# Grouped whitening in one pass: centring y on its mean over all samples before the gram, against correcting for the mean in the solve

## The reference

```python
y = gn(x)                       # per sample, 32 groups of 4 channels: (v - mean) / sqrt(var + 1e-5)
xf = transpose(y, (1, 0, 2, 3)).reshape(128, M)          # M = 32*56*56
mu = mean(xf, axis=1);  xc = xf - mu
xg = xc.reshape(16, 8, M)                                # 16 groups of 8 channels
cov = einsum('gim,gjm->gij', xg, xg) / M + 1e-4 * eye(8)
e, v = eigh(cov);  proj = v @ diag(rsqrt(e)) @ v.T       # the inverse square root
out = x + (proj @ xg).reshape(C, M) * weight + bias      # back in NCHW
```

## Time and profile before

| | |
|---|---|
| median of 3 runs | 427.79 us (425.38 to 430.95) |
| profiled execution, its own time | 428.58 us |
| its span, first to last instruction | 426.8 us |
| mean granted TensorE clock | 0.994 of full speed |
| bytes moved by DMA | 103.76 MB, mean 243 GB/s |

### The profile page before, as it was taken

How to read it: one execution, slowest core, us unless ns; L and a number is a source line. 1 busy time by engine, 2 the same in 40 slices (tenths; PEclk the granted TensorE clock), 3 DMA queues, 4 the chain that set the end, 5 groups by cost and what they waited for, 6 DMA issues and landing times.

```text
span 426.8 us, 9162 instructions
## 1 busy us (share of the span) xinstructions
PE 359.5 (84%) x3394; PEld 226.6 (53%) x3394; DVE 337.5 (79%) x885; ACT 327.4 (77%) x513; POOL 300.3 (70%) x196
## 2 busy tenths in 40 slices
PE   0124667999999999999999999999999999999991
PEld 0013555565656656655666565656565656555450
DVE  2689999689899999999999999999999885732000
ACT  1065766498989898998989898989898989865462
POOL 0079999387888979797878787878787888930000
PEclk9999999999999999999999999999999999999997
DMA  6999999247766975787776877677866999373657
GB/s 224 275 327 332 315 302 299 80 152 213 236 229 231 294 219 180 243 277 225 229 244 221 294 231 233 233 257 258 283 222 214 328 340 330 121 229 130 226 178 274
DMA packets 18892, 103.76 MB, mean 243 GB/s; under 512 B 6432, under 2 KB 6432, under 8 KB 14752
## 3 DMA queue, kind: packets, MB, share of 16 engines
q1 hardware_dynamic: 18848, 103.19, 74.2%
HBM read 51.78 MB, written 51.38 MB: 242 GB/s over the span
## 4 chain that ended last, share of the span: by engine, by line
PE 47%; POOL 19%; DVE 14%; ACT 8%; issue 6%; SPq 3%; DMA 1%; DVEq 0%
PE ps_apply L564 32%; POOL hl_ring L330 15%; PE ps_small L564 7%; PE ps_gram L564 5%; DVE a_t L445 5%; POOL ring L322 5%; ACT hl_ring L516 4%; ACT ring L525 3%; SPq L286 3%; PE ps_stat L564 3%; DVE bn L346 3%; DMA ring<-in_x_dram 1%; DVE t_ring L392 1%; DVE entries L441 1%; DVE var L362 1%
## 5 line engine op out<-in xcount | busy, mean ns | idle before, releaser
L330 POOL TENSOR_TENSOR hl_ring<-ring,hl_ring 128x768 f16<-128x768 f32 (+1 forms) x128 | 236.4, 1860 | 52.3 <-ACT hl_ring L516 52.2
L564 PE MATMUL ps_apply<-ring,a_t 128*128 128x392 f32 x512 | 203.3, 522 | 0.0
L516 ACT CAST hl_ring<-ring 128x768 f16<-128x768 f32 (+1 forms) x128 | 135.4, 1075 | 10.9 <-POOL ring L322 10.3
L525 ACT ACTIVATE ring<-ps_apply,fin_add,scale 128x784 f32<-128x784 f32 x128 | 126.2, 996 | 20.8 <-PE ps_apply L564 20.7
L346 DVE BATCH_NORM_STATS2 bn<-ring 128x6 f32<-128x448 f32 x224 | 128.7, 595 | 9.8 <-DMA ring<-in_x_dram 9.8
L392 DVE STREAM_TRANSPOSE t_ring<-hl_ring 128x768 f32<-128x768 f32 (+1 forms) x128 | 125.9, 984 | 3.6 <-POOL hl_ring L330 2.0
L564 PEld LDWEIGHTS ps_apply<-ring,a_t 128*128 128x128 f32 x512 | 88.0, 191 | 42.3 <-ACT ring L525 2.3
L564 PE MATMUL ps_gram<-t_ring 128*128 128x64 f16 x1568 | 74.6, 200 | 16.9 <-DVE t_ring L392 16.9
L322 POOL TENSOR_SCALAR ring<-ring,y_mul,y_add 128x832 f32<-128x832 f32 x64 | 66.8, 1044 | 25.8 <-DVE dr L384 25.1
L564 PEld LDWEIGHTS ps_gram<-t_ring 128*128 128x128 f16 x1568 | 61.6, 103 | 26.7 <-DVE t_ring L392 18.3
L504 ACT ACTIVATE ring<-ring,y_add,y_mul 128x768 f32<-128x768 f32 x64 | 65.3, 1020 | 0.0
(11 more groups left out here) (65 smaller groups left out, 228.8 us busy)
## 6 DMA issues: line engine op xcount, KB each, us to landing
ring<-in_x_dram SPq DMA_DIRECT2D x256, 196.0 KB, 3.7
out_dram<-ring SPq DMA_DIRECT2D x128, 392.0 KB, 5.0
cst<-const_dram SPq DMA_DIRECT2D x1, 392.0 KB
wb<-in_L_conv_weight_dram SPq DMA_DIRECT2D x1, 0.5 KB
wb<-in_L_conv_bias_dram SPq DMA_DIRECT2D x1, 0.5 KB
```

The costliest lines, as they stand in the source:

```text
L330: nc.gpsimd.tensor_tensor(hl[:, :, 0], ring[:, g % RING, s, px], hl[:, :, 1], ALU.subtract).then_inc(l_ready, 1)
L516: nc.scalar.copy(hl_ring[:, i % HL_RING, 0:width(p), 1], ring[:, g % RING, s, px]).then_inc(h_ready, 1)
L525: nc.scalar.activation(ring[:, g % RING, s, px].rearrange("p (a b) -> p a b", a=2), ps_apply[:, i % 2 * 2:i % 2 * 2 + 2, 0:BANK], ACT.Iden ...
L564: return nc.tensor.matmul(out_, lhsT, rhs, start=start, stop=stop, skip_group_check=True)
```

## The change

The mean of y over all samples is computed before y is made. It needs only the rows' means: `dr` is multiplied by a new constant matrix `every`, which sums over all rows of the same channel modulo 8 and gives each row its channel's mean. The new step `centre` subtracts it from the shift of y (`y_add`) and makes the result's bias `fin_add` at once. With y centred, `HOP_MU`, `HOP_SHIFT`, the `wmu` product and the mean's outer product in `HOP_COV` go; 19 hops are left. `HOP_COV` leaves a plain 8x8 matrix and the first step builds the 16-row layout from it with four products of 8 rows (`cov` and `p0` padded with zeros, `eye`). The addition of the identity writes PSUM (`s_entries`), and `a_t` is expanded from there. All lists of ticks are other ones.

```diff
-ROWS, DEV, VAR, VAREPS, SCALED, Y_SET, STAT_OPS = 2, 3, 6, 7, 10, 12, 13
+ROWS, DEV, VAR, VAREPS, SCALED, DR, Y_SET, STAT_OPS = 2, 3, 6, 7, 10, 13, 14, 15
-BN_AT = [-64, -60, -56, -51, -44, -42, -37, -33, -31, -23, -19, -18, -18, -14]
+BN_AT = [-65, -59, -54, -50, -44, -41, -35, -32, -32, -25, -21, -21, -15, -11]
 MEAN_PE_AT = 1
-DEV_AT = 2
-VAR_PE_AT = 4
-VAREPS_AT = 6
-ROOT_AT = 8
-SCALE_AT = 13
-Y_POOL = {0: 18, 2: 19, 4: 47, 6: 56}
-Y_ACT = {1: 28, 3: 38, 5: 56, 7: 70}
-H_AT = [20, 32, 40, 42, 44, 56, 71, 77]
-L_AT = [31, 42, 48, 49, 50, 69, 75, 82]
-T_AT = [36, 42, 50, 60, 70, 75, 83, 95]
-GRAM_AT = [41, 47, 56, 65, 72, 79, 87, 96]
+DEV_AT = 3
+VAR_PE_AT = 5
+VAREPS_AT = 7
+ROOT_AT = 9
+SCALE_AT = 14
+MU_AT = 16
+CENTRE_AT = 20
+Y_POOL = {0: 9, 2: 23, 4: 47, 6: 66}
+Y_ACT = {1: 21, 3: 33, 5: 47, 7: 72}
+H_AT = [27, 31, 40, 42, 52, 53, 74, 80]
+L_AT = [19, 28, 31, 50, 58, 68, 71, 81]
+T_AT = [36, 44, 52, 65, 70, 79, 84, 96]
+GRAM_AT = [41, 48, 57, 65, 73, 80, 88, 100]
-HOP_AT = [95, 103, 108, 111, 115, 117, 124, 129, 132, 136, 140, 145, 151, 152, 156, 160, 166, 168, 170, 178, 185]
+HOP_AT = [103, 106, 110, 115, 121, 124, 129, 131, 135, 138, 144, 147, 150, 154, 159, 166, 169, 171, 177]
-HOP_READ_AT = [102, 106, 110, 114, 115, 122, 126, 130, 134, 138, 141, 146, 150, 154, 158, 162, 168, 169, 174, 179,
-               188]
+HOP_READ_AT = [104, 108, 115, 116, 123, 127, 130, 134, 139, 142, 146, 152, 154, 159, 162, 166, 169, 174, 181]
-APPLY_AT = [189, 196, 206, 212, 219, 229, 236, 244]
-FINISH_AT = [197, 200, 207, 220, 223, 238, 241, 260]
-STORE_AT = [222, 262]
+APPLY_AT = [192, 198, 206, 213, 220, 229, 236, 248]
+FINISH_AT = [196, 205, 211, 222, 228, 235, 241, 255]
+STORE_AT = [224, 257]
...
+    put("every", (p[:, None] % CG == p[None] % CG) / N)
...
-                nc.vector.scalar_tensor_tensor(out=y_add[:, i], in0=s_mean, scalar=-1.0, in1=y_mul[:, i],
+                nc.vector.scalar_tensor_tensor(out=y_shift[:], in0=s_mean, scalar=-1.0, in1=y_mul[:, i],
                                                op0=ALU.mult, op1=ALU.mult).then_inc(stat_step, 1)
-                nc.vector.tensor_tensor(dr[:, i], dev, y_mul[:, i], ALU.mult).then_inc(stat_step, 1)
+                nc.vector.tensor_tensor(dr[:], dev, y_mul[:, i], ALU.mult).then_inc(stat_step, 1)
+
+            def centre(g):
+                i = g % STAT_RING
+                dve.wait_ge(stat_mm, STAT_MMS * g + 3)
+                mu = s_mu.broadcast_to([P, TILES])
+                nc.vector.tensor_tensor(y_add[:, i], y_shift[:], mu, ALU.subtract).then_inc(stat_step, 1)
+                nc.vector.scalar_tensor_tensor(out=fin_add[:, i], in0=mu, scalar=1.0, in1=scale[:, i],
+                                               op0=ALU.mult, op1=ALU.mult).then_inc(centred, 1)
+                dve.wait_ge(centred, g + 1)
+                nc.vector.tensor_tensor(fin_add[:, i], fin_add[:, i], base[:], ALU.add).then_inc(stat_step, 1)
...
-                    nc.vector.tensor_copy(wmu[:, e], s_wmu[e]).then_inc(solve_read[e], 1)
                     dve.wait_ge(a_step, MATRIX_STEPS * g + 2)
-                    nc.vector.tensor_tensor(entries[:, 1], entries[:, 0],
-                                            k_("id8").unsqueeze(1).broadcast_to([P, TILES, CG]),
+                    whole = s_entries[e].rearrange("p (s c) -> p s c", s=TILES)
+                    nc.vector.tensor_tensor(whole, entries[:], k_("id8").unsqueeze(1).broadcast_to([P, TILES, CG]),
                                             ALU.add).then_inc(a_step, 1)
                     dve.wait_ge(a_step, MATRIX_STEPS * g + 3)
                     nc.vector.tensor_tensor(a_t[:, e].rearrange("p s (n c) -> p s n c", c=CG),
-                                            entries[:, 1].unsqueeze(2).broadcast_to([P, TILES, SAMPLES, CG]),
+                                            whole.unsqueeze(2).broadcast_to([P, TILES, SAMPLES, CG]),
...
+            def mean_of_rows(g):
+                pe.wait_ge(stat_step, STAT_OPS * g + DR)
+                for s in range(TILES):
+                    ins = product(s_mu, k_("every"), dr[:, s:s + 1], s == 0, s == TILES - 1)
+                ins.then_inc(stat_mm, 1)
...
+                if k == HOP_COV:
                     if g >= 2:
-                        pe.wait_ge(fin_ready, g - 1)
+                        pe.wait_ge(a_step, MATRIX_STEPS * (g - 1))
                     pe.wait_ge(gram_reduced, g + 1)
+                    product(s_cov[e], k_("sel"), g_red[:, e], True, False)
+                    ins = product(s_cov[e], g_red[:, e], k_("sel"), False, True)
+                if k == HOP_WV[0]:
+                    c, p = cov[:, e], p0[:, e]
+                    product(s_w[e], c[:, CG:], p[:, 0:CW], True, False)
+                    product(s_w[e], eye[:, 0:CW], p[:, CG:], False, True)
+                    product(s_v_[e], eye[:, CG:], p[:, 0:CW], True, False)
+                    ins = product(s_v_[e], c[:, 0:CW], p[:, CG:], False, True)
```

More of the change, by code:

```diff
@@ L52 @@
 ITERS = len(POLY)
[L57 to L62, removed]
+HOP_COV = 0
+HOP_M = [None] + [2 * k for k in range(1, ITERS)]
+HOP_WV = [2 * k + 1 for k in range(ITERS)]
+HOP_T = 2 * ITERS
+HOP_V, HOP_ROOT = HOP_T + 1, HOP_T + 2
+HOPS = HOP_T + 3
 READS = HOPS - 1
 CW = 2 * CG
-ROWS, DEV, VAR, VAREPS, SCALED, Y_SET, STAT_OPS = 2, 3, 6, 7, 10, 12, 13
+ROWS, DEV, VAR, VAREPS, SCALED, DR, Y_SET, STAT_OPS = 2, 3, 6, 7, 10, 13, 14, 15
@@ L95 @@
+APPLY_AT = [192, 198, 206, 213, 220, 229, 236, 248]
+FINISH_AT = [196, 205, 211, 222, 228, 235, 241, 255]
+STORE_AT = [224, 257]
 LOAD_AT = [STORE_AT[s] + 24 - RING * TICKS for s in range(TILES)]
-FIRST_TICK, LAST_TICK = -TICKS, TICKS * (GROUPS - 1) + 264
+FIRST_TICK, LAST_TICK = -65, TICKS * (GROUPS - 1) + 259
 COLS = {}
 _at = 0
-for _name, _w in (("avg", P), ("bmask", P), ("gmask", UNIT), ("sel", 8 * CG), ("id8", CG),
-                  ("means", 11 * CG), ("expand", P), ("eps", CG), ("eye15", CG), ("wv0", 2 * CW),
+for _name, _w in (("avg", P), ("bmask", P), ("gmask", UNIT), ("sel", CG), ("id8", CG),
+                  ("every", P), ("expand", P), ("eps", CG), ("eye", 3 * CG), ("eye15", CG),
@@ L120, in constants @@
         / (N * HW * Y_SCALE ** 2))
-    sel = np.zeros((P, 8 * CG))
-    sel[:, 3 * CG:4 * CG] = sel[:, 4 * CG:5 * CG] = ch[:, None] % CG == np.arange(CG)[None]
-    put("sel", sel)
+    put("sel", ch[:, None] % CG == np.arange(CG)[None])
     put("id8", p[:, None] % CG == np.arange(CG)[None])
[L125 to L129, removed]
+    put("every", (p[:, None] % CG == p[None] % CG) / N)
     put("expand", p[None] % CG == np.arange(CG)[:, None])
@@ L180, in zca_residual @@
         zx = sb("zx", [CG, 2, P])
-        wmu = sb("wmu", [CG, 2, 1])
-        entries = sb("entries", [P, 2, TILES, CG])
+        entries = sb("entries", [P, TILES, CG])
         a_t = sb("a_t", [P, 2, TILES, P])
-        fin_add = sb("fin_add", [P, 2, TILES])
+        fin_add = sb("fin_add", [P, STAT_RING, TILES])
         ps_apply = ps("ps_apply", [P, 4, 512])
@@ L403, in gram_sum @@
                 dve.wait_ge(gram_masked, g + 1)
-                blocks = g_red[:, g % 2, 3 * CG:5 * CG].rearrange("p (b i) -> p b i", i=CG)
-                nc.vector.tensor_reduce(blocks, g_masked[:].rearrange("p (n i) -> p i n", i=CG).unsqueeze(
-                    1).broadcast_to([P, 2, CG, CG]), AX.X, ALU.add).then_inc(gram_reduced, 1)
+                nc.vector.tensor_reduce(g_red[:, g % 2], g_masked[:].rearrange("p (n i) -> p i n", i=CG),
+                                        AX.X, ALU.add).then_inc(gram_reduced, 1)
             def read_hop(g, k):
@@ L449, in read_hop @@
                                             ALU.mult).then_inc(a_step, 1)
[L450 to L454, removed]
             def read_weights():
                 dve.wait_ge(wb_product, 1)
-                nc.vector.tensor_scalar(wb[:, :, 0], s_wb[:, 0:GROUPS], -1.0 / TRACE ** 0.5, None, ALU.mult)
-                nc.vector.tensor_scalar(wb[:, :, 1], s_wb[:, 0:GROUPS], 1.0 / (Y_SCALE * TRACE ** 0.5), None,
+                nc.vector.tensor_scalar(wb[:, :, 0], s_wb[:, 0:GROUPS], 1.0 / (Y_SCALE * TRACE ** 0.5), None,
                                         ALU.mult).then_inc(w_scaled, 1)
-                nc.vector.tensor_copy(wb[:, :, 2], s_wb[:, GROUPS:2 * GROUPS])
+                nc.vector.tensor_copy(wb[:, :, 1], s_wb[:, GROUPS:2 * GROUPS])
                 dve.wait_ge(w_scaled, 1)
-                nc.vector.tensor_tensor(id8w[:], wb[:, :, 1].unsqueeze(2).broadcast_to([P, GROUPS, CG]),
+                nc.vector.tensor_tensor(id8w[:], wb[:, :, 0].unsqueeze(2).broadcast_to([P, GROUPS, CG]),
                                         k_("id8").unsqueeze(1).broadcast_to([P, GROUPS, CG]),
                                         ALU.mult).then_inc(wb_ready, 1)
-            nc.vector.memset(g_red[:], 0.0).then_inc(zeros_set, 1)
+            nc.vector.memset(cov[:], 0.0)
+            nc.vector.memset(p0[:], 0.0).then_inc(zeros_set, 1)
```

(11 more changed lines are left out.)

73 lines of the change are left out of this document (27 added, 46 removed).

## The result

The changed kernel takes 449.19 us (447.98 to 449.89) against 426.95 beside it, ratio 1.0503 [1.0424, 1.0581]. Forecast were 412 us and 404 to 423. The profiled execution took 449.57 us with a span of 447.8.

What follows compares the result with a forecast made beforehand. Bound: the chain of waits through `a_t`, 22.39 us a period, with TensorE nearly full. 22.39 - 1.63 + 0.5 gave 21.3, larger than TensorE's 20.86; 13.1 us over 12 periods, 15.9 in total, hence 412 us, range 404 to 423.

Steps and rivals of the forecast that it cites:

- `a_t` from PSUM: VectorE's expansion into `a_t`, with one PSUM input, escapes the wait for GpSimd: 1.63 us a period saved.
- TensorE's work: TensorE's busy time in a period falls by a net 0.84 us, from 21.52 to 20.68.
- The mean product's wait: TensorE, before the new mean product, should wait 0 to 0.3 us for `dr`.
- the late shift: `y_add` comes later, so GpSimd's first normalisation starts 0.8 us later, covered by its 3.61 us idle a period.
- The addition of `base`: VectorE's third instruction in `centre`, both inputs in SBUF, waits about 1.0 us for a GpSimd normalisation.
- The addition of the identity: VectorE's L441, still with two SBUF inputs, waits for GpSimd between 0 and 1.66 us.
- Rival C: Both VectorE additions wait for a whole GpSimd subtraction, 3.7 us together, and hold TensorE: slower, 441 us; chance 0.05.
- Rival B: The wait passes to L441 or the `base` addition, which catches a 1.8 us subtraction: period 22.0, 422 us; chance 0.17.
- TensorE's floor: The shortest period TensorE allows: its work of 20.68 plus 0.18 us of remaining idle time, 20.86 us.
- rival A: TensorE is not the limit and the chain of waits shortens in full: period 20.76, 406 us; chance 0.20.
- the 0.5 us of mean products: The new mean products lie in the TensorE stretch that the chain of waits crosses, adding 0.5 us a period.
- SP's places: Stores move by 2 to 5 ticks in SP's DMA queue, at no cost while ring slots have slack.

Runs made afterwards that it cites:

- e2: The kernel before with only the PSUM part: the addition of the identity writes PSUM and `a_t` is expanded from there; 415.82 us, 0.9736.
- e5: e1 with the product `entries` in PSUM too, so that the addition of the identity has one SBUF input; 415.66 us, 0.9724 against the kernel before.
- e1: The changed kernel with `id8w` kept in PSUM and `spread_in` placed right before `g_masked`; 420.03 us, 0.9793 against the kernel before.
- e9: e5 with the load of a ring slot 36 ticks later in SP's queue; 405.12 us, 0.9479 against the kernel before.
- e8: The kernel before with `SUM_AT` 101 instead of 99, so a transposition comes between `g_masked` and `spread_in`; 479.34 us, 1.1215.
- e3: The changed kernel with 8 unread products of 96 columns on TensorE just before its wait for `g_red`; 432.68 us, 1.0121 against the kernel before.
- e7: The changed kernel with `SUM_AT` 99 instead of 103, `spread_in` right behind `g_masked`; 431.65 us, 1.0116 against the kernel before.

## Why the prediction was wrong, point by point

- **`a_t` from PSUM** (1.63 us off `a_t`): right. All 16 take 424 ns, also beside GpSimd (e2, e5), and e2 alone gives 2.6%. The surcharge for a PSUM source in the Trainium skill (VectorE: DVE Perf Modes, TRN2 errata) does not show: 424 against 424.
- **TensorE's work** 20.68: right, 20.72 in e1 and 20.65 in e5.
- **The mean product's wait** (0 to 0.3 us) and **the late shift** (0.8 us, covered): right. TensorE shows no wait before the mean product at 181.68, GpSimd waits 0.58 for `y_add`, and neither costs anything in e9.
- **The addition of `base`** (1.0 us of lock): wrong, 184 ns. It starts at 182.58, 0.01 before the normalisation that I had it wait for, and is not held. **The addition of the identity** (0, at most 1.66) took 184 ns, since GpSimd was idle.
- **The step that failed** is the list of what the lock can catch. I priced the two additions whose operands the change touches and wrote that "every queue is reordered", but did not go through the two-input instructions that are merely moved. `spread_in` was one: its 162 to 168 ns in twelve steady periods looked like a harmless instruction, where they showed only that it fell into 1.1 us of GpSimd's idle time. `SUM_AT` was moved behind a transposition by the change, and this was there to be read. The runs showed 1.58 us for it instead of 0.17, and a wait of 1.63 us a period on TensorE.
- **The second failed term** is the clock. The sum has none. Beside the 1.63 us of wait it took another 1.6 a period. Without it the kernel would have been about as fast as before (22.34 against 22.39 a period), and not 5% slower.
- **Rival C** had the kind (lock waits that hold TensorE) and the sign, with a chance of 0.05, on the wrong instructions and at 441 us. Its condition, 3.4 us of lock a period, was wrong: 1.4 us lay on the path to the covariance hop and not beside it, and with the clock that was enough. **Rival B** (the lock handed on) is what e1 shows, for 0.9 us.
- **The forecast's own period** of 21.3 is that of e1, 21.24, but by luck: e1 contains a lock of 0.9 us on the addition of the identity that the sum put at nothing. Without it the period is 20.90 (e5, e9), which is what the sum called TensorE's floor, 20.86, and **rival A** had. So the 0.5 us of mean products, added to the chain, did not count in full, and the larger of the two terms was the wrong one. The Trainium skill, Perfetto Trace Analysis, Identifying the Most-Contended Engine, would have TensorE short of its limit by its weight-load share. The runs disagree here: e2 and e9 end at its matmul busy time, 21.44 of 21.61 and 88.92 of 90.00 us, with weight loads at 62% and 60%.
- **SP's places "cost nothing"**: true at 22.4 us a group and false at 20.90 (e5 against e9, 10.5 us); in e1, at 21.24, the statistics also wait for a load.

## What to carry to other kernels

Before moving an instruction of VectorE that reads two SBUF tensors, look at what GpSimd runs at its new place; its old duration says where it stood, not what it is. Give it one input in PSUM or a place where the GpSimd instruction that runs is about to end. On a TensorE that is nearly full, price a new wait in a stretch of tiny products at twice its length, as here, until the clock row says otherwise, and after every gain look for the next queue that is outrun, here the loads.

## What the runs showed of the hardware that was not expected

- A VectorE instruction of 16 elements with two SBUF inputs waits for the rest of the GpSimd instruction that runs: 1.58 and 1.07 us in the rows above, each ending with the subtraction, and 1.76 in e8. With one input in PSUM it takes 0.15 beside a normalisation (e1) and 0.18 in the middle of a subtraction (e5). The Trainium skill, SBUF — State Buffer, Who interferes with whom, says that such an instruction contends with a GpSimd instruction that reads SBUF, that one with at most one SBUF input does not, and that the order of issue decides who blocks. The rows agree, and the `base` addition, 0.01 us earlier than the normalisation and not held, fits too.
- TensorE's clock fell from 2.4 to 1.2 GHz after a wait of 1.63 us that stood in a stretch of tiny products: 3.8 us from the end of one apply unit to the next (188.6 to 192.4). It did so in every steady period but the first with this wait, at 94.4 to 98.0, where the same instructions and the same wait left it at 1.00. It stayed up when products of 96 columns filled the wait (e3) and over the 0.69 us wait between apply units of the kernel before.
- What tips it is not settled. The same stretch did and did not lower it in the changed kernel. In e7 such a stretch is 2.52 us (160.26 to 162.78), with 0.36 us of a marked wait, and the clock falls in some periods; in e5 it is 2.14 us and stays up; in the kernel before it is 2.53 us (204.84 to 207.37), nearly without a gap and with products of 48 columns in it, and stays up. Length and filling were not varied one by one.
